# A two-phase attention and mixture-of-experts layer on one core: the product with V as one segment on TensorE

## What is computed

```python
qkv = (x @ W_qkv + b_qkv).reshape(B, S, 3, H, hd)         # H = 16 heads of hd = 32
q, k, v = (qkv[:, :, 0], qkv[:, :, 1], qkv[:, :, 2])
attn = jnp.einsum('bqhd,bkhd->bhqk', q, k) / jnp.sqrt(jnp.asarray(hd, x.dtype))
attn = jax.nn.softmax(attn, axis=-1)
attn_out = jnp.einsum('bhqk,bkhd->bqhd', attn, v).reshape(B, S, D)
...
return attn_out + moe_out
```

## Time and profile before

| | us |
|---|---|
| median of three runs (1523.93 to 1524.84) | 1524.28 |
| span of the profiled execution, first to last instruction | 1509.8 |
| PE busy, share of the span | 1338.6, 89% |
| DVE busy | 972.3, 64% |
| ACT busy | 913.0, 60% |
| POOL busy | 378.7, 25% |
| one half of a product (16 passes of L990) | 1.92 |
| one exponential, L694 | 0.66 |
| one turned exponential, L704 | 1.03 |

### The profile page before, as it was taken

How to read it: one execution, slowest core, us unless ns; L and a number is a source line. 1 busy time by engine, 2 the same in 40 slices (tenths; PEclk the granted TensorE clock), 3 DMA queues, 4 the chain that set the end, 5 groups by cost and what they waited for, 6 DMA issues and landing times.

```text
span 1509.8 us, 25299 instructions
## 1 busy us (share of the span) xinstructions
PE 1338.6 (89%) x6912; PEld 989.5 (66%) x6913; DVE 972.3 (64%) x2077; ACT 913.0 (60%) x1842; POOL 378.7 (25%) x592
## 2 busy tenths in 40 slices
PE   5989999998689999999999999999985768899976
PEld 4958888887665656656566565665652347677765
DVE  4247777776668977777777777777766643333332
ACT  4123333342368889888898888988985643333322
POOL 0002222221000031011110111101145036667665
PEclk9899999999699999999999999999996689999998
DMA  5013222228252543435434354343455187678766
GB/s 153 1 63 106 98 97 97 97 90 280 69 147 63 124 109 66 130 78 126 105 65 127 80 126 105 63 127 82 98 123 117 32 241 137 121 145 156 136 124 106
DMA packets 96813, 166.46 MB, mean 110 GB/s; under 512 B 25339, under 2 KB 33659, under 8 KB 95459
## 3 DMA queue, kind: packets, MB, share of 16 engines
q1 hardware_dynamic: 64992, 113.69, 26.8%
q0 software_dynamic: 27136, 46.23, 17.7%
q10 hardware_dynamic: 4611, 5.74, 1.5%
HBM read 62.71 MB, written 52.58 MB: 76 GB/s over the span
## 4 chain that ended last, share of the span: by engine, by line
PE 57%; DMA 14%; DVE 9%; issue 8%; ACT 6%; POOL 4%; POOLq 1%; ACTq 0%; DVEq 0%; SPq 0%
PE banks L208 10%; DMA out_dram<-plain,score_bias 10%; PE banks L210 10%; PE banks L209 10%; PE banks L990 8%; PE banks L954 5%; PE banks L974 5%; DVE plain L1438 3%; ACT plain L704 2%; ACT banks L694 2%; POOL plain L547 1%; DMA h_rows<-plain 1%; POOL out_dram L559 1%; PE banks L867 1%; PE banks L934 1%
## 5 line engine op out<-in xcount | busy, mean ns | idle before, releaser
L208 PE MATMUL banks<-parts 128*128 128x512 f32 (+6 forms) x1108 | 436.2, 394 | 32.9 <-DVE plain L1527 9.0
L209 PE MATMUL banks<-parts 128*128 128x512 f32 (+6 forms) x1108 | 421.1, 380 | 0.0
L210 PE MATMUL banks<-parts 128*128 128x512 f32 (+6 forms) x1108 | 421.0, 380 | 0.0
L1438 DVE TENSOR_REDUCE plain<-banks 128x1 f32<-128x512 f32 x512 | 329.3, 683 | 62.3 <-PE banks L954 59.1
L694 ACT ACTIVATE banks<-banks,plain 128x512 f32<-128x512 f32 x512 | 339.2, 663 | 46.6 <-DVE plain L1438 43.9
L704 ACT ACTIVATE plain<-banks 128x1024 f32<-128x1024 f32 x256 | 262.6, 1026 | 40.0 <-PE banks L974 32.7
L208 PEld LDWEIGHTS banks<-parts 128*128 128x128 f32 (+1 forms) x1108 | 212.9, 192 | 76.2 <-issue 36.1
L210 PEld LDWEIGHTS banks<-parts 128*128 128x128 f32 (+1 forms) x1108 | 212.3, 192 | 39.9
L209 PEld LDWEIGHTS banks<-parts 128*128 128x128 f32 (+1 forms) x1108 | 213.4, 193 | 33.9
L954 PE MATMUL banks<-parts 96*128 96x512 f32 x512 | 207.5, 444 | 26.6 <-ACT banks L694 25.7
L974 PE MATMUL banks<-parts 104*128 104x512 f32 x512 | 176.9, 427 | 25.6 <-ACT plain L704 24.6
(11 more groups left out here) (184 smaller groups left out, 1634.0 us busy)
## 6 DMA issues: line engine op xcount, KB each, us to landing
parts<-parts SPq DMA_DIRECT2D x384, 128.0 KB, 2.3
plain<-in_x_dram SPq DMA_DIRECT2D x32, 256.0 KB, 2.6
out_dram<-plain SPq DMA_DIRECT2D x32, 256.0 KB, 2.0
h_rows<-plain SPq DMA_DIRECT2D x32, 256.0 KB, 2.0
parts<-h_rows SPq DMA_DIRECT2D x8, 1024.0 KB, 5.5
parts<-plain SPq DMA_DIRECT2D x8, 1024.0 KB, 4.6
out_dram<-plain POOLq DMA_DIRECT2D x16, 512.0 KB
parts<-expert_weights ACTq DMA_DIRECT2D x4, 1024.0 KB, 17.5
```

What stands on the lines that cost most here:

```text
L208: pe.matmul(out, stat[0], mov[0], start=first, stop=False)
L209: pe.matmul(out, stat[0], mov[1], start=False, stop=False)
L210: return pe.matmul(out, stat[1], mov[0], start=False, stop=last)
L1438: dve.tensor_reduce(nmx[:, k, t:t + 1], bank[SB[t]][:], AX.X, ALU.max, negate=True).then_inc(q["f_max"], 1)
```

## The change

In the two kinds of step with a product, the pieces PVa and PVb stand next to each other, behind S3 and T0@1. In the plain PV step S3 and T0@1, which stood between and behind the halves, move ahead of both. In the PV H step S3 moves from behind PVb to a place ahead of PVa, and H2 from between the halves to behind H1; H3, which was last, is still last. The strings of ACT and DVE are the same as before.

```diff
-            "PV": {"pe": "T2@2 S0 n@1 S1 S2 PVa S3 T0@1 PVb",
+            "PV": {"pe": "T2@2 S0 n@1 S1 S2 S3 T0@1 PVa PVb",
                    "act": "t2@2 E3@1 E0 E1 t0@1 E2 PV",
                    "dve": "s@1 n@1 D@1 m0 m1 m2 m3"},
-            "PV H": {"pe": "T2@2 S0 n@1 S1 H0 S2 T0@1 H1 PVa H2 PVb S3 H3",
+            "PV H": {"pe": "T2@2 S0 n@1 S1 H0 S2 T0@1 H1 H2 S3 PVa PVb H3",
                      "act": "t2@2 H0 E3@1 H1 E0 t0@1 H2 E1 E2 H3 PV",
                      "dve": "s@1 D@1 n@1 H0 m0 H1 m1 m2 H2 m3"}}
```

## The result

| | before | after |
|---|---|---|
| median of the runs | 1524.11 us (1521.8 to 1524.84) | 1571.72 us (1564.38 to 1572.26) |
| ratio, 95% interval | 1 | 1.0307 (1.0291 to 1.0323) |
| profiled execution: span | 1509.8 us | 1569.8 us |
| profiled execution: own time | not recorded | 1571.55 us |

The change costs 47.6 us on the medians. The forecast was 1568 us in a range of 1543 to 1590: slower by 43.9 us. The sign and the size are right. What follows asks whether the parts of the sum are right too. Three of them were off, in opposite directions, so that the nearness of the total is partly luck.

The account below looks back on a forecast made before the run. PE was taken to bound the kernel, with ACT almost level and each waiting on the other. Plain steps 7.8, PV H steps 13.6 and clock falls 22.5 sum to 43.9 us: 1524.3 + 43.9 = 1568 us, range 1543 to 1590.

Parts of the forecast that it names:

- The plain step: Plain PV step on PE: S3 waits uncovered for E3@1, 0.65 us lost, 0.25 saved, +0.40; all 23 places 7.8 us.
- E3@1: Plain PV step: the previous head's fourth exponential on ACT, which S3 was to wait for, 0.65 us lost.
- The saving: Plain PV step on PE: fewer passages between product halves and other matmuls, segment 4.36 us, 0.25 us saved.
- The PV H step: Batches 0 to 6: H2 waits 1.4 us for H1's bank, ACT's queue delays H3; +1.94 us, 7 places, 13.6 us.
- The clock: PE's granted clock falls where waits thin its work: 15 of 26 places at 1.5 us, 22.5 us.
- The last batch: Its two plain places, beside weight copies and partly at low clock: bounds -0.25 and +0.4 each, taken as 0.
- what lies around the span: The 14.5 us between span and median, taken to lie outside the first and last instruction and left unchanged.
- The clock holds: Rival, whole kernel: no clock falls, only the waits count, 21.4 us, so 1545.7 us; chance 0.24.
- Fewer passages: Rival, 30 places: S3 doesn't wait, each keeps the 0.25 us saved, -7.5 us, 1516.8 us; chance 0.05.
- Absorbed: Rival: later slack on ACT and PE takes the waits; wholly 1524 us, chance 0.03; in part 1538 us, chance 0.06.

Follow-up runs that it names:

- the filled kernel: Changed kernel plus matmuls nobody reads, four between S2 and S3, five between H1 and H2 (not in the last batch): 1552.71 us, ratio 1.0222.
- the unchanged run: The kernel before, nothing edited, timed and profiled a second time: 1520.6 us, ratio 0.9994; span 1520.6 us.
- both kernels on the third: Against before: plain step joined behind T0 and T1, 1527.97 us; that plus PV H joined directly behind H1, 1537.13 us.

## Why the prediction was right, and where it was not

**The plain step.** Right in its cause: S3 waits for E3@1, 0.66 us against 0.65. The saving was mis-sized. The prediction took S3 to T0 as 0.23 us, the price of a second matmul in a row; behind a wait it takes 0.34 (892.48 to 892.82), and the segment 4.47 instead of 4.36. So 0.14 us is saved against the order of before, not 0.25, and the place costs 0.52, not 0.40. On 19 places that is 9.9 us instead of 7.4. Moving S3 alone, with the halves left apart, costs 0.84 us a place, so the joining as such does save 0.3 us; the uncovered wait takes more than that away. By the Trainium skill (TensorEngine Tiling (Array Packing), Key Properties) a change of tiling mode drains the engine. The timelines agree in that one way into and out of the product more costs 0.33 us (4.80 against 4.47), about 0.1 at each change of instruction; the uncovered wait of 0.66 is twice the whole of it.

**The PV H step.** Right in each step: the wait of 1.40 us, H3's delay by way of ACT's queue, and the sum of 1.95 against 1.94. The two experiments on it confirm both links apart: with the product as a cover, the 1.40 us vanish (+1.0 stays, by H3's bank), and with ACT's order adapted the second link goes.

**The clock.** Right that it falls, and that it is about four tenths of the cost. The term was 15 falls at 1.5 us, 22.5; there are 12, and by the filled kernel each costs 1.55, together 18.6. So the price was right and the count a guess that came out three too high. It was the weakest step: the PV H steps, thinner by their rows, brought two falls in seven places when changed alone, the plain steps nine in 21; in the changed kernel it was four in seven and seven in 21. Which of two like places falls stays open; it depends on more than the place.

By the Trainium skill (Perfetto Trace Analysis, Matmul Optimizations) matmuls should run back to back in batches. The trace agrees only in part: the 32 passes are back to back, and the clock falls nevertheless, at waits ahead of them. The rule was met inside the segment and broken in front of it.

**The last batch and what lies around the span.** Both assumptions were wrong. From its first product to its last, the last batch takes 97.3 us against 91.4 in the unchanged run, +5.9, where the prediction had 0 for its two places. This can't be split cleanly: the stall there has 17.4 us on ACT in the unchanged run (7.75 + 9.68) and 20.0 in the changed one (14.45 + 5.57), and the clock is low for long stretches in both. Nor is all of it shown to be the change's: the kernel with the PV H step alone takes 91.3 us there and the one with ACT's order adapted 94.6, though in the last batch, which has no H pieces, both have the same orders.

```profile
1181.44 1.02 ACT L704 ACTIVATE plain<-banks 128x1024 f32<-128x1024 f32 x1 [14.45 <-remote]
...
1189.38 0.59 ACT L709 COPY plain<-banks 128x512 f32<-128x512 f32 x1 [5.57 <-remote]
```

**The sum as measured**, on the spans of the changed and the unchanged run (49.2 us). The seven batches grow by 41.3, of which 18.6 is the clock and 22.7 waits. Before the first product lie 1.8 us; the first PV H step is there, whose product comes 2.29 us later behind H1 (461.03 to 463.91 against 461.57 to 462.16), and the start varies by itself by 3 us between the two traces of before. The last batch has 5.9, the end 0.2. So 24.5 us of waits, 18.6 of clock and about 6 of the last batch stand against 21.4, 22.5 and 0. The clock was taken 4 us too dear, the waits and the last batch 9 us too cheap. That these errors partly cancel, and that the forecast so came within 4 us of the median, is luck.

**The rivals.** "The clock holds" (1545.7 us) is what the filled kernel comes near to. It costs 31.9 us on the medians and 26.9 on the spans (1547.5 against 1520.6) where this rival had 21.4; its two falls and 2.9 us more in the last batch account for the difference on the spans. In the changed kernel the clock does not hold. "Fewer passages" fell because S3 does wait. "Absorbed" fell because the period of a batch without a fall grows by 3.57 us (842.74 to 940.87 is 98.13), all of 3 x 0.52 + 1.95 = 3.51.

```profile
842.74 3.64 PE L990 MATMUL banks<-plain,parts 128*32 128x512 f32 x32
...
940.87 3.64 PE L990 MATMUL banks<-plain,parts 128*32 128x512 f32 x32
```

## What to carry to other kernels

A piece of work between two waiting instructions is a cover: before moving it, read when the instruction behind it could start without it, and whose queue stands behind the wait. Where the granted clock falls near such a wait, the wait has a second price, here 1.55 us for every fall on top of costs of 0.5 to 2 us a place; test it by filling the gap with work that does nothing. And profile the unchanged kernel twice: if a span lies much farther below the time of its runs than another kernel's does, its trace does not show all that the runs have.

## What the runs showed of the hardware that was not expected

A PE instruction that follows one that had waited comes about 0.1 us later than it does in a running stream: 0.34 instead of 0.23 us from S3 to T0, 0.67 instead of 0.56 from T0 to PVa. The first matmul behind a product is like it, without a wait: 0.34 from S3 to T0. No bracket shows this tenth.

In the last batch ACT, PE and DVE stop together in most profiled executions, released by nothing that the trace records; ACT stands there in two stretches of 5.6 to 14.5 us. It is in all eight traces taken for this study on the first two chips and in that of the changed kernel, absent from both kernels on the third, where before itself is 11 us quicker, and from the recorded trace of before. These three have one stretch of 8.8 to 11.0 us instead, in which ACT waits for DVE (L1438). A transfer of 16 KB on an instruction queue begins within 1 us of the start of the stall in the unchanged run (1124.7) and in the changed one (1167.8); in before one begins at 1121.8, and nothing stops with it. The cause is open, and no run here was made on it.
